# Graph aggregation: steps of a node block accumulate in one PSUM bank, ScalarE builds the selections, VectorE copies finished blocks

## The reference, cut to what matters

```
def _sage_layer(h, edge_src, edge_dst, W, b, inv_deg):
    msgs = h[edge_src]
    agg = jax.ops.segment_sum(msgs, edge_dst, num_segments=h.shape[0]) * inv_deg
    y = jnp.concatenate([h, agg], axis=1)
    return y @ W + b
...
h = _sage_layer(x, edge_src, edge_dst, W1, b1, inv_deg)
h = jax.nn.relu(h)
h = _sage_layer(h, edge_src, edge_dst, W2, b2, inv_deg)
```

## Time and profile before

| | us |
|---|---|
| runs | 9305.02, 9308.93, 9310.25 |
| median | 9308.93 |
| profiled execution | 9304.79 |
| its span | 9303.0 |

### The profile page before, as it was taken

The page is one execution under the profiler, slowest core; times in us unless marked ns, Lnnn a source line. Parts: engine busy times, 40 slices in busy tenths (PEclk is TensorE's granted clock), DMA queues, the critical chain, the costliest instruction groups (busy, mean ns, idle before and its releaser), DMA issues. The chain is left out here.

```text
span 9303.0 us, 136379 instructions
## 1 busy us (share of the span) xinstructions
PE 4981.6 (54%) x23720; PEld 4235.1 (46%) x23721; DVE 5226.4 (56%) x14857; ACT 3069.6 (33%) x6894; POOL 6343.5 (68%) x6767
## 2 busy tenths in 40 slices
PE   1444434446444444345566666666646666666664
PEld 0333333335444433333455555555425555555552
DVE  5333333334433333336577777777757777777776
ACT  2000000002000000003466666666416666666653
POOL 4777777772777777776577777777217777777761
PEclk8666556657556666667677767777776777777777
DMA  6222222225222222224555555555255555555543
GB/s 124 63 63 63 63 62 62 63 61 170 63 63 61 63 63 63 61 63 122 156 165 161 165 160 165 161 165 161 81 174 163 161 166 161 165 161 165 161 136 111
DMA packets 626359, 1087.90 MB, mean 117 GB/s; under 512 B 211481, under 2 KB 394810, under 8 KB 625870
## 3 DMA queue, kind: packets, MB, share of 16 engines
q0 software_dynamic: 261920, 645.88, 25.0%
q1 hardware_dynamic: 257678, 361.65, 12.6%
q10 hardware_dynamic: 106400, 77.09, 2.8%
HBM read 980.84 MB, written 103.25 MB: 117 GB/s over the span
## 5 line engine op out<-in xcount | busy, mean ns | idle before, releaser
L1494 POOL DMA_INDIRECT conv_kv<-key_value,conv_src x3328 | 3184.5, 957 | 1404.0 <-issue 973.9
L727 POOL DMA_INDIRECT second_msg<-sage_hidden_projected,second_src x1564 | 1491.1, 953 | 625.4 <-issue 473.6
L727 POOL DMA_INDIRECT first_msg<-sage_in,first_src x1564 | 1487.8, 951 | 535.4 <-issue 465.6
L1715 PE MATMUL conv_ps_sums<-conv_kv,conv_sel 128*128 128x136 f32 x6656 | 1302.9, 349 | 542.6 <-DVE sums L1643 501.4
L1701 PE MATMUL conv_ps_query<-query_table,conv_selT 128*128 x6656 | 1358.8, 368 | 268.3 <-issue 150.4
L1715 PEld LDWEIGHTS conv_ps_sums<-conv_kv,conv_sel 128*128 128x128 f32 x6656 | 1135.8, 246 | 676.1 <-DVE sums L1643 658.8
L1701 PEld LDWEIGHTS conv_ps_query<-query_table,conv_selT 128*128 128x128 f32 x6656 | 1195.0, 266 | 356.9 <-issue 342.4
L1643 DVE TENSOR_TENSOR sums<-sums,conv_ps_sums 128x136 f32 x3328 | 972.6, 292 | 462.5 <-PE conv_ps_sums L1715 138.1
L821 PE MATMUL first_ps_sums<-first_msg,first_sel 128*128 x3328 | 727.5, 399 | 669.8 <-ACTq L747 508.5
L1780 ACT ACTIVATE conv_sel<-iota_row,conv_rel 128x128 f32<-128x128 f32 x3328 | 1051.8, 386 | 55.0 <-PE conv_ps_sums L1715 54.3
L821 PE MATMUL second_ps_sums<-second_msg,second_sel 128*128 x3328 | 721.2, 397 | 623.6 <-ACTq L747 452.6
(11 more groups left out here) (238 smaller groups left out, 5069.8 us busy)
## 6 DMA issues: line engine op xcount, KB each, us to landing
conv_place<-place_rows SPq DMA_DIRECT2D x416, 512.0 KB
conv_kv<-key_value,conv_src POOLq DMA_INDIRECT x3328, 2.9
first_msg<-sage_in,first_src POOLq DMA_INDIRECT x1564, 2.5
second_msg<-sage_hidden_projected,second_src POOLq DMA_INDIRECT x1564, 2.5
conv_pen<-run_penalties SPq DMA_DIRECT2D x416, 48.5 KB
sage_own_hidden<-first_own_out ACTq DMA_DIRECT2D x49, 256.0 KB
sage_dense_own<-sage_own_hidden SPq DMA_DIRECT2D x14, 896.0 KB
sage_hidden_transposed<-sage_dense_hid SPq DMA_DIRECT2D x14, 896.0 KB
```

Of the source, the lines that this page charges most:

```text
L727: pool.indirect_dma_start(msg[:, j * MW:j * MW + D], None, table, bass.IndirectOffsetOnAxis(ap=src[:, b, j:j + 1], axis=0)).then_inc(gathe ...
L1494: pool.indirect_dma_start(kv[:, h * CH + j, :], None, t.kv_d, bass.IndirectOffsetOnAxis(ap=src[:, h, j:j + 1], axis=0)).then_inc(gathered[ ...
L1715: last = pe.matmul(sums_of(h, step), sel[:, k % SELG, step % GR, :], kv[:, h * CH + step, DEN:2 * D], start=True, stop=True)
```

## The change

It touches setup (two tables more) and `sage_edges` (both aggregation phases).

- PSUM has four banks (`SUM_BANKS`). A step's matmul adds into the bank of its block (block number modulo four), with `start=False`; the bank was set to zero before. TensorE reads place and bank from two tables into registers.
- VectorE no longer selects and no longer adds. For each of the 98 blocks it waits until the block's last group of steps is made, copies the bank to `sums` and sets the bank to zero (`flush`). `sums` is no longer cleared as a whole.
- ScalarE builds the selections with four `Abs` and one `Relu` activation per group (`build`), and does TensorE's waits (`release`): for the tiles, for a free bank, for the selection. It then raises `sel_ready`, the only thing TensorE waits for in a group.
- SyncE takes over the waits for landings, and frees a ring group once the group eight further on has landed and its own last use is done.
- Setup writes `bank_of_step` (1664 numbers) and `last_step_group_of_block` (98 numbers), with one more `iota` of 1664 elements on GpSimd and six more operations on VectorE.

```
@@ setup, SyncE
-                    for table, rows_i in ((t.slot_d, slot), (t.need_d, need), (t.last_d, lastuse)):
+                    for table, rows_i in ((t.slot_d, slot), (t.need_d, need), (t.last_d, lastuse), (t.bank_d, bank)):
                         sp.dma_start(table.rearrange("(j p) -> p j", p=P), rows_i[:, :],
                                      allow_slow_non_contiguous=True).then_inc(steps_out, 16)
-                    sp.wait_ge(steps_out, 112)
+                    sp.wait_ge(steps_out, 128)
...
+                    sp.wait_ge(ends_ready, 1)
+                    sp.dma_start(t.end_d.rearrange("(p a) -> p a", a=1), endg[0:NB, :],
+                                 allow_slow_non_contiguous=True).then_inc(tables_out, 16)
@@ setup, GpSimd and VectorE
+                pool.iota(tile[:, :], [[1, STEPS]], 0, 0, allow_small_or_imprecise_dtypes=True).then_inc(iotas, 1)
...
-                dve.wait_ge(iotas, 4)
+                dve.wait_ge(iotas, 5)
...
+                link(dve.tensor_tensor(below[:, :], fbc[:, :], tile[:, :], ALU.subtract))
+                link(dve.tensor_scalar(tile[:, :], below[:, :], part[:, 0:1], 0.0, ALU.is_le, ALU.add, accum_out=upto[:, :]))
...
@@ sage_edges, SyncE
+                def landed(k, half):
+                    sp.wait_ge(gathered[k], 16 * GR * half + 16 * GR)
+                    sp.sem_inc(tiles_in, 1)
+
+                def half_lap(half, first):
+                    for k in range(RG):
+                        landed(k, half)
+                        if k >= BEHIND or not first:
+                            last = sp.value_load(lastuse[0:1, bass.ds(half * RG + (k - BEHIND), 1)],
+                                                 min_val=0, max_val=STEPS // GR - 1)
+                            sp.wait_ge(sums_ready, last + 1)
+                            sp.sem_inc(place_free, 1)
@@ sage_edges, ScalarE
+                def release(c, k):
+                    top = act.value_load(newest[0:1, bass.ds(c * KG + k, 1)], min_val=0, max_val=NB - 1)
+                    if k % (EARLY // GR) == 0:
+                        tiles = act.value_load(need[0:1, bass.ds(c * (CH // EARLY) + k * GR // EARLY, 1)],
+                                               min_val=0, max_val=GROUPS - 1)
+                        act.wait_ge(tiles_in, tiles + 1)
+                    act.wait_ge(bank_free, top + 1)
+                    act.wait_ge(sel_built, KG * c + k + 1)
+                    act.sem_inc(sel_ready, 1)
+
+                def build(c, h, k, used):
+                    if used is not None:
+                        act.wait_ge(sums_ready, KG * used + k + 1)
+                    lo = h * CH + k * GR
+                    for i in range(GR):
+                        act.activation(sel[:, lo + i, :], t.iota[:, :], ACT.Abs,
+                                       bias=rel[:, bass.ds(c * CH + (k * GR + i), 1)], scale=-1.0).then_inc(away_ready, 1)
+                    act.wait_ge(away_ready, CH * c + (GR * k + GR))
+                    act.activation(sel[:, lo:lo + GR, :], sel[:, lo:lo + GR, :], ACT.Relu, bias=1.0,
+                                   scale=-1.0).then_inc(sel_built, 1)
+
+                def chunk(n, h, used):
+                    for k in range(KG):
+                        release(n, k)
+                        build(n + 1, 1 - h, k, used)
@@ sage_edges, VectorE
+                def flush(block, b):
+                    end = dve.value_load(ends[0:1, bass.ds(block, 1)], min_val=0, max_val=STEPS // GR - 1)
+                    dve.wait_ge(sums_ready, end + 1)
+                    chain.link(dve.tensor_copy(t.acc[:, bass.ds(block * MW, MW)], ps[:, b * 512:b * 512 + MW]))
+                    dve.memset(ps[:, b * 512:b * 512 + MW], 0.0).then_inc(bank_free, 1)
@@ sage_edges, TensorE
-                        pe.wait_ge(sel_ready, n)
-                        pe.wait_ge(ps_used, n)
+                        pe.wait_ge(sel_ready, g * (2 * KG) + (h * KG + k + 1))
                         for i in range(GR):
...
+                            j = (k * GR + i) % (CH // 2)
+                            last = pe.matmul(ps[:, bass.ds(to[j] * 512, MW)], sel[:, h * CH + k * GR + i, :],
+                                             msg[:, bass.ds(at[j] * MW, MW)], start=False, stop=False, skip_group_check=True)
```

More of the change, by code:

```diff
@@ L194, in setup_phase @@
         slot = sb("slot", [P, SJ], I32)
+        bank = sb("bank", [P, SJ], I32)
+        tile = sb("tile", [P, STEPS])
+        upto = sb("upto", [P, 1])
+        ended = sb("ended", [P, 1])
+        endi = sb("endi", [P, 1], I32)
+        endg = sb("endg", [P, 1], I32)
         need = sb("need", [P, SJ], I32)
@@ L749, in _ @@
-                lap(0)
-                with act.Fori(1, 2 * LAPS - 1) as g:
-                    lap(g)
-                lap(2 * LAPS - 1)
-                own.scalar(act, (4 * LAPS, 0, 2 * LAPS))
-                for k in range(REST):
-                    act.wait_ge(gathered[k], 16 * GR * (2 * LAPS + 1))
-                    act.sem_inc(tiles_in, 1)
-                own.scalar(act, (4 * LAPS + 1, 1, 2 * LAPS))
+                def release(c, k):
[7 more added lines that the diff above has]
+                    act.sem_inc(sel_ready, 1)
@@ new lines, in chunk, with pair @@
+                def chunk(n, h, used):
+                    for k in range(KG):
+                        release(n, k)
+                        build(n + 1, 1 - h, k, used)
+                def pair(g):
+                    for h in range(2):
+                        n = g * 2 + h
+                        own.scalar(act, (n, h, g))
+                        chunk(n, h, n - 1 if not (isinstance(n, int) and n == 0) else None)
+                act.wait_ge(rel_in, 16)
+                act.wait_ge(need_in, 32)
@@ L758, in _ @@
+                for k in range(KG):
+                    build(0, 0, k, None)
+                pair(0)
+                with act.Fori(1, 2 * LAPS - 1) as g:
+                    pair(g)
+                pair(2 * LAPS - 1)
+                pair(2 * LAPS)
+                for n in range(4 * LAPS + 2, NC_ - 1):
+                    chunk(n, n % 2, n - 1)
+                for k in range(KG):
+                    release(NC_ - 1, k)
                 own.finish(act)
@@ L789, in _ @@
-                for k in range(KG):
-                    select(0, 0, k)
-                dve.memset(t.acc[:, :], 0.0).then_inc(sums_set, 1)
-                dve.sem_inc(ps_used, 2)
-                dve.wait_ge(blk_in, 16)
-                dve.wait_ge(sums_set, 1)
-                with chain.turns(PAIRS - 1, 2 * CH) as g:
-                    add_up(g * 2, 0, g * 2 + 1)
-                    add_up(g * 2 + 1, 1, g * 2 + 2)
-                add_up(NC_ - 2, 0, NC_ - 1)
-                add_up(NC_ - 1, 1, None)
+                for b in range(SUM_BANKS):
+                    dve.memset(ps[:, b * 512:b * 512 + MW], 0.0).then_inc(bank_free, 1)
@@ L801, in _ @@
+                dve.wait_ge(ends_in, 16)
+                with chain.turns(NB // SUM_BANKS, SUM_BANKS) as g:
+                    for b in range(SUM_BANKS):
+                        flush(g * SUM_BANKS + b, b)
+                first = NB // SUM_BANKS * SUM_BANKS
+                for b in range(NB - first):
+                    flush(first + b, b)
             @block.tensor
             def _(pe):
-                regs = [pe.alloc_register(f"{tag}_slot{i}") for i in range(CH // 2)]
+                places = [pe.alloc_register(f"{tag}_slot{i}") for i in range(CH // 2)]
@@ L804, in _, with loaded @@
+                banks = [pe.alloc_register(f"{tag}_bank{i}") for i in range(CH // 2)]
                 pe.wait_ge(ones_set, 1)
                 pe.wait_ge(slot_in, 32)
+                def loaded(regs, tab, at, top):
+                    pe.load(regs, tab[0:1, bass.ds(at, len(regs))])
+                    return [pe.snap(r, min_val=0, max_val=top) for r in regs]
                 def chunk_sums(g, h):
+                    c2 = g * 4 + 2 * h
                     for k in range(KG):
+                        q = k // (KG // 2)
```

102 lines of the change are left out of this document (41 added, 61 removed).

## The result

The changed kernel takes 9253.78 us by the median of 5 runs (9248.84 to 9257.46), the kernel before 9307.29 (9303.9 to 9310.25, 5 runs). The ratio is 0.9943 with a 95% interval of 0.9928 to 0.9957: 53.5 us less. I had forecast 9257. The profiled execution took 9253.78 us too, with a span of 9252.0 against 9303.0.

The account below looks back on a forecast made before the run. GpSimd's gathers, one after the other at 1.25 us a tile, were taken as the bound. Terms -26.1 - 10.4 - 25.3 + 10.3 = -51.5 us took 9304.79 to 9253.3; with 4.1 for the median, 9257, range 9240 to 9287.

Parts of the forecast that it names:

- (a): Both aggregation phases: with selections off VectorE, no gather is stretched above the median; -26.1 us, bounds nothing and 26.1.
- Rival A: Aggregation phases: gathers stay stretched, any work beside them being the cause; 9283 us, chance 0.12.
- (b): Ring of gathered tiles: ScalarE's lag goes and GpSimd no longer waits for a place; -10.4 us, bounds nothing and 10.4.
- (c): Phase ends: the tail after the last gather's start falls from 30.1 and 11.2 to 8.0 us each; -25.3 us.
- Rival B: Ring and tails: the lag stays in another form through ScalarE's single order; 9276 to 9292 us, chance 0.09.
- (d): ScalarE's new load in the phases: 5.2 us a pair of groups, 27.5 us a chunk against GpSimd's 37.6; hidden.
- Rival D: Phases: ScalarE sets the pace if a pair of groups costs over 7.7 us; some 10120 us, chance 0.05.
- (e): Phases: TensorE's extra register loads, the 98 copies and memsets are hidden; clearing `sums` gives nothing.
- (f): Setup: a sixth table costs 9.2 us, iota 1.0, one more chained operation 0.1; together +10.3 us.
- rival C: Setup: the new table costs 18.1 us instead of 9.2, 9266 us; free, 9248; chance counted in the forecast's 0.70.
- Rival E: Phases: DMA landings alone set pace and tails, so only setup's 10.3 us shows; 9319 us, chance 0.04.

Follow-up runs that it names:

- e2: The kernel of e1 with the selections moved to ScalarE too; additions, partial sums and setup as in the kernel before: 9255.1 us, ratio 0.9938.
- e4: Changed kernel with 17 idle VectorE operations behind each block copy, two SBUF inputs in `first`, one in `second`: 9453.78 us, one run.
- e1: Kernel before, with SyncE taking landings in ring order and ScalarE none; selections and additions stay on VectorE: 9288.02 us, ratio 0.9972.
- the dose: Changed kernel with idle `Abs` on ScalarE, four more a group in `first`, eight in `second`: 12,590 us, one run, when everything was slower.
- e12: The kernel before, unchanged, profiled once more: 9310.72 us.
- e3: Changed kernel with setup's near loads put ahead of five of the step tables: 9258.27 us, ratio 0.9942.
- e11: Changed kernel with near loads as in e3, `setup_tile` iota last, block-end chain and its table behind the records: 9251.44 us, ratio 0.9945.
- e7: The kernel of e11, run on chip A when everything was slower: 12,330 us, ratio 1.0265.
- e9: The kernel of e11, run on chip B when everything was slower: 12,101 us, ratio 1.0235.

## Why the prediction was right, step by step

The time came out 3 us from the forecast, and the sum of the terms, -51.5, beside a measured -51.0 of the span. That the sum is this close is in part luck: the setup cost 2.5 us less than its term, and the dense part and all behind the second phase, for which there was no term, 4.9 us more. And the median fell on the profiled execution, 9253.78, where I had put it 4.1 us above.

**(a) Stretched gathers, forecast -26.1.** Measured 27.7, by the sums of the gathers (1487.8 + 1491.1 to 1475.6 twice). That VectorE's selections did it is shown: e2 takes them away and keeps the additions, which it clears, and e4's `first` brings them back. That it takes two inputs from SBUF is not shown, since e4's one-input operation holds gathers too. Rival A is out, and with it the first place that the probe in the Trainium skill, "SBUF — State Buffer", section "Who interferes with whom", would have given it; with the rule's other half, that two SBUF inputs contend with a GpSimd instruction that reads SBUF, e4's `first` agrees (2120.3 us against 1951.0). The 957 ns of the conv layers, which spoke for A, have the same source: in the kernel before all 192 gathers over 1.0 us there start inside an operation of VectorE. The size holds only in the kernel before. Once the landings are in order, taking the same selections away gave 37.1.

**(b) The ring, forecast -10.4.** The waits went, by the cause named (e1). Alone this is worth 0.6 us (1970.1 + 1969.8 to 1966.9 + 1972.4), since GpSimd then meets more selections: 641 gathers start inside one, in place of 499, and 182 instead of 108 of them 0.05 to 0.5 us into it. (a) and (b) together, -36.5, measured -37.9. Their sum holds because both were removed; I had priced each as if it stood alone.

**(c) The tails, forecast -25.3 to 8.0 us each.** Measured 7.9 and 7.6, -25.8. e1 has 9.7 and 8.8 with the additions kept, so all but some 3 us of it is the order on SyncE and ScalarE, not VectorE's lighter work. Rival B is out.

**(d) ScalarE, forecast hidden, 5.2 us a pair.** In the 27 places of `first` where it goes from one pair to the next with at most 1.1 us of idle time, a pair takes 4.7 to 5.6 us, and 5.2 in the rows above. ScalarE waits 820.4 us for tiles in `first`, 178 times in 208 pairs; that it would be every pair was too much. Rival D, which needs 7.7, did not come true. How much more load it would have taken was not measured, since the dose ran when everything was slower.

**(e) TensorE, copies, clearing of the sums, forecast 0.** e2 and the changed kernel have the same stretch within 0.1 us.

**(f) Setup, forecast +10.3.** Measured +7.8 in the first pair of profiles, 6.0 by the means of all. The mis-sized term is the table: I divided the whole stretch of five tables by five, 9.2. Five take 45.8, 46.6, 47.6 and 48.4 us from the first issue to the near loads (before, e12, e1, e2), six take 52.9 and 53.4 (the changed kernel, e4), and `tile_of_step` alone 12.2 (e3). So the sixth adds 6.1 us by the means, where four of the five cost 34.9, 8.7 each; why the last is cheaper, no run shows. It lies within rival C's bounds. The chain of the block ends is hidden only behind this loss (e3).

Rival E is out: the gathers' pace moved.

## What to carry to other kernels

Where GpSimd's gathers set the pace, look for VectorE operations beside them whose tensor inputs all lie in SBUF, and see where in them the gathers start; such work did no harm here on ScalarE, nor with one input in PSUM. One input in place of two is not enough. A semaphore that is passed on by an engine with work of its own lags by that engine's order: let the idle queue do it. And before two gains that use the same engine's time are added, undo them one at a time, since here the removal of the ring waits alone was worth 0.6 us of the gathers' stretches.

## What the runs showed of the hardware

- Selections that stand alone stretch 116 of 499 gathers that start inside one; in rows without gaps, 789 of 821, most from 0.94 to 1.15 us. All that start 0.05 to 0.5 us into a selection are held in the kernel before (108), and end 0.81 to 0.83 us after it.
- A one-input operation on SBUF (`tensor_scalar`, 128x512, 0.41 us) holds a gather in the same way (4 of 4), and 677 of 1666 took about 0.69 us behind a gather that had started first (e4). No gather was held by the additions with one input in PSUM (671 start inside one in e2).
- In the three profiles in which a write of 98 single elements stands among the large writes at the end of setup (e11, e7, e9), it is 29.5 to 30.8 us from the first of them to the next phase's load, and 23.3 to 24.3 us in the others.
- One chip ran the kernel before in 12,021 us at one time and in 9,305 us later. In the slower condition the changed kernel's operations were as long as ever (a gather 943 ns, an `Abs` 392) with gaps put down to nothing between them, and the order of the two kernels turned round.
